# State-space stage of a transformer kernel: scan results transposed on TensorE and weighted by C columns on their way out of PSUM

## The reference, cut to what matters

```python
x = jnp.einsum('ed,bld->bel', in_proj_w, hidden_states)
xc = conv(x, conv_w)                       # depthwise, 4 taps
u = jax.nn.silu(xc + conv_b)
x_dbl = jnp.einsum('ke,bel->bkl', x_proj_w, u)
dt_lo, Bm, Cm = x_dbl[:, :DR], x_dbl[:, DR:DR + DS], x_dbl[:, DR + DS:]     # DR = 8, DS = 16
delta = softplus(einsum('er,brl->bel', dt_proj_w, dt_lo) + dt_proj_b)
A = -jnp.exp(A_log)
def step(state, xs):                       # over the 256 tokens; state is (b, 256 channels, 16)
    d_t, B_t, C_t, u_t = xs
    state = state * jnp.exp(d_t[..., None] * A) + (d_t * u_t)[..., None] * B_t[:, None, :]
    return state, jnp.einsum('ben,bn->be', state, C_t)
y = (scan of step) + D[None, :, None] * u
y = y * jax.nn.silu(z)
x = x + tanh(g_xattn[0]) * swap(y)
```

## Time and profile before

| | us |
|---|---|
| median of 3 runs | 1043.12 |
| lowest, highest | 1041.15, 1044.63 |
| span of the profiled execution (first to last instruction) | 1042.2 |
| of it, the state-space stage up to the next stage's first instruction | 160.2 |
| of that, first scan to end of last scan | 39.7 to 150.8 |

### The profile page before, as it was taken

The page is one execution under the profiler, slowest core; times in us unless marked ns, Lnnn a source line. Parts: engine busy times, 40 slices in busy tenths (PEclk is TensorE's granted clock), DMA queues, the critical chain, the costliest instruction groups (busy, mean ns, idle before and its releaser), DMA issues. The chain is left out here.

```text
span 1042.2 us, 16671 instructions
## 1 busy us (share of the span) xinstructions
PE 871.7 (84%) x5342; PEld 522.6 (50%) x5348; DVE 726.8 (70%) x1420; ACT 582.1 (56%) x1113; POOL 384.8 (37%) x329
## 2 busy tenths in 40 slices
PE   9456566989999999999499488999749999957787
PEld 4122223643577777777277373333425666645445
DVE  5999996788866676666768768997452324138875
ACT  5534442588677777777466365888403343205462
POOL 0366640068545555454133172000012766310132
PEclk9699997999999999999799899999969999979989
DMA  3321107400000000000000100400294332240001
GB/s 97 124 80 61 60 1 285 159 11 11 12 20 15 20 21 17 20 15 6 5 1 2 57 1 14 151 23 2 59 347 125 71 78 44 36 116 1 1 0 42
DMA packets 44348, 57.64 MB, mean 55 GB/s; under 512 B 5672, under 2 KB 35120, under 8 KB 44288
## 3 DMA queue, kind: packets, MB, share of 16 engines
q1 hardware_dynamic: 37792, 48.72, 13.9%
q0 software_dynamic: 4416, 6.03, 3.5%
q10 hardware_dynamic: 2080, 2.10, 0.6%
HBM read 50.29 MB, written 6.49 MB: 54 GB/s over the span
## 5 line engine op out<-in xcount | busy, mean ns | idle before, releaser
L1345 POOL TENSOR_TENSOR a_scratch<-a_scratch,a_inverse 128x512 f32<-128x512 f32 x64 | 66.5, 1039 | 115.3 <-DVE a_inverse L1481 115.3
L521 POOL TENSOR_TENSOR ssm_drive<-ssm_du,ssm_b_row 128x1024 f32<-128x1024 f32 x31 | 72.9, 2351 | 66.0 <-DVE ssm_state L596 33.2
L392 PE MATMUL bank<-ssm_seen,ident 128*128 128x512 f32 x128 | 63.3, 619 | 24.9 <-DVE ssm_seen L606 24.9
L2558 PE MATMUL bank<-wup,moe_xT 128*128 x184 | 83.0, 594 | 1.2 <-issue 0.6
L2342 DVE TENSOR_REDUCE a_tops<-bank 128x4 f32<-128x1024 f32 x64 | 77.7, 1223 | 8.5 <-PE bank L2022 5.5
L2793 DVE TENSOR_TENSOR moe_act_f<-bank,moe_silu 128x512 f32<-128x512 f32 x23 | 15.9, 692 | 92.7 <-ACT moe_silu L2627 80.6
L479 ACT ACTIVATE bank<-ssm_delta,ssm_a_neg 128x510 f32<-128x510 f32 x64 | 44.1, 690 | 63.7 <-DVE ssm_state L596 63.7
L2190 ACT ACTIVATE wup<-bank,a_exp_scale 128x1024 f32<-128x1024 f32 x64 | 71.1, 1113 | 13.8 <-PE bank L2045 13.8
L596 DVE TENSOR_TENSOR_SCAN ssm_state<-bank,ssm_drive 128x512 f32<-128x512 f32 x64 | 74.8, 1210 | 2.9 <-POOL ssm_drive L521 0.2
L1264 ACT ACTIVATE a_scratch<-bank,a_bias,a_q_factor 128x256 f32<-128x256 f32 x128 | 71.1, 559 | 7.1 <-DVE a_bias L1468 6.8
L1076 PE MATMUL bank<-keys,a_scratch 128*128 (+1 forms) x256 | 69.1, 392 | 1.6 <-DVE xn L1408 0.7
(11 more groups left out here) (499 smaller groups left out, 2203.6 us busy)
## 6 DMA issues: line engine op xcount, KB each, us to landing
ssm_b_row<-ssm_b_spill SPq DMA_DIRECT2D x16, 512.0 KB, 3.6
wup<-in_l_up_dram SPq DMA_DIRECT2D x8, 1024.0 KB, 9.5
a_wq_in<-in_l1x_q_dram SPq DMA_DIRECT2D x32, 128.0 KB, 2.1
wdn<-in_l_down_dram SPq DMA_DIRECT2D x8, 512.0 KB, 10.5
keys<-in_l1x_o_dram SPq DMA_DIRECT2D x1, 2048.0 KB, 10.9
X<-in_x_dram SPq DMA_DIRECT2D x1, 1024.0 KB, 6.9
lora_raw<-in_l_gate_dram SPq DMA_DIRECT2D x1, 1024.0 KB, 6.9
lora_raw<-in_l_up_dram SPq DMA_DIRECT2D x1, 1024.0 KB, 8.9
```

The source lines that it names most:

```text
L392: last = pe.matmul(bank[:, 4 + 2 * k + h, :], core.ident[:, :], seen[:, k, h * HALF:(h + 1) * HALF], start=False, stop=m >= STEPS - CC, sk ...
L521: pool.tensor_tensor(drive[:, k, :], du[:, k, :], b_row[:, n % NROW, :], ALU.mult).then_inc(S["drive_ready"], 1)
L1345: pool.tensor_tensor(prob[:, j, :, :], prob[:, j, :, :], inverse[:, j, :].unsqueeze(2).to_broadcast([P, 2, SEQ]), ALU.mult).then_inc(S["p_ ...
L2558: last = pe.matmul(bank[:, 2 * (i % 2) + m, :], xT[:, i % 2, c, :], wup[:, bass.ds(e, 1), c * 2 * FF + m * FF:c * 2 * FF + (m + 1) * FF] . ...
```

## The change

- Each unit of a column is now turned: TensorE transposes four 128x128 pieces of `state` (two tiles of 128 tokens by two chunks), a "round", into one PSUM bank (`turn`, banks 2 and 3 in turns). A column has four rounds. Time then stands on partitions, so that C is a column of factors, one per partition (`c_cols`, made once by eight small transposes and one copy on ScalarE).
- The bank is emptied through a multiplication by that column: rounds 0, 1 and 2 by ScalarE in two activations of 128x256 with a per-partition scale, round 3 by VectorE in one 128x512 multiplication (`weigh`). In the last column VectorE takes round 2 as well.
- `gather` adds the result with one 512-column matmul per round. The sum stands with time on partitions, so the transposes at the end go, and the skip term is now 16 matmuls of 128 columns.
- `c_rows`, the three bf16 parts and the load of the selection matrix go. So does `see`.
- z: GpSimd normalises the eight tiles behind drives 6 to 13 (`normal`). TensorE turns them in four extra rounds, one behind each of the columns 8 to 11, ScalarE copies them out (`bring_z`), and applies silu at the end. VectorE multiplies sum, gate and silu(z) into `gated`, and GpSimd adds that to `X`.
- `drive` has four buffers, `state` four (two columns by two chunks), `seen` four of half the size.

```diff
-    NROW = 4
+    NROW, NDRIVE, NSEEN = 4, 4, 4
     STEPS = CC * NS
+    ROUNDS = NT // 2
+    Z_STEP = 8
...
-select3 = s.sb("select3", [96, NS * P], BF16)
-parts, minus = s.sb("parts", [96, NTOK], BF16), s.sb("minus", [P, P], BF16)
-sixteenth, nmean, log_var = s.sb("sixteenth", [P, 1]), s.sb("nmean", [P, NT]), s.sb("log_var", [P, NT])
+c_cols = s.sb("c_cols", [P, NS, NT])
+sixteenth, log_var = s.sb("sixteenth", [P, 1]), s.sb("log_var", [P, NT])
...
-drive = s.sb("drive", [P, 2, NTOK])
-state = s.sb("state", [P, 2, NTOK])
-seen = s.sb("seen", [P, 2, NTOK])
+drive = s.sb("drive", [P, NDRIVE, NTOK])
+state = s.sb("state", [P, 2, CC, NTOK])
+seen = s.sb("seen", [P, NSEEN, HALF])
...
-silu_z = s.sb("silu_z", [P, NT, DM])
+z_turned = s.sb("z_turned", [P, NT // 2, HALF])
+gated = s.sb("gated", [P, NT // 2, HALF])
...
+rounds = []
+for n in range(NS):
+    rounds += [(n, r) for r in range(ROUNDS)] + [(n, "z")] * (Z_STEP <= n < Z_STEP + ROUNDS)
+place = {q: i for i, q in enumerate(rounds)}
+by_vector = lambda q: q[1] == 3 or q == (NS - 1, 2)
+emptied = {q: sum(by_vector(o) == by_vector(q) for o in rounds[:place[q] + 1]) for q in rounds}
+ring = lambda q: 2 + place[q] % 2
+def await_emptied(engine, q):
+    engine.wait_ge(S["dve_emptied" if by_vector(q) else "act_emptied"], emptied[q])
...
-        sp.dma_start(select3[:, :], d["select3"][:, NS * P:2 * NS * P]).then_inc(S["s_s"], 16)
...
-        pe.wait_ge(S["minus_ready"], 1)
-        for i in range(2):
-            rows = slice(2 * NS * i, 2 * NS * (i + 1))
-            pe.wait_ge(S["part_ready"], i + 1)
-            pe.wait_ge(S["rows_ready"], 1)
-            for h in range(2):
-                last = pe.matmul(bank[0:2 * NS, 2 + h, :], minus[rows, rows], parts[rows, h * HALF:(h + 1) * HALF],
-                                 start=False, stop=True, skip_group_check=True)
-            last.then_inc(S["part_out"], 1)
-        pe.wait_ge(S["part_ready"], 3)
-        pe.wait_ge(S["s_s"], 16)
-        def c_rows(n):
-            if n >= 1:
-                pe.wait_ge(S["seen_ready"], CC * n)
...
-        def gather(m):
-            k = m % CC
-            pe.wait_ge(S["seen_ready"], m + 1)
...
-        c_rows(0)
-        for n in range(NS):
-            gather(CC * n)
-            if n + 1 < NS:
-                c_rows(n + 1)
-            gather(CC * n + 1)
-        for b in range(NB):
-            pe.wait_ge(S["y_ready"], 3 + b // 2)
-            for h in range(2):
+        def skip_term(r):
+            for t in (2 * r, 2 * r + 1):
                 for k in range(CC):
-                    last = pe.transpose(bank[:, b, h * DM + k * P:h * DM + (k + 1) * P],
-                                        seen[:, k, b * SEQ + h * P:b * SEQ + (h + 1) * P], core.ident[:, :])
-            last.then_inc(S["y_turned"], 1)
+                    at = t % 2 * DM + k * P
+                    pe.matmul(bank[:, 4 + r, at:at + P], u[:, k, t * P:(t + 1) * P], skip_diag[:, k, :],
+                              start=t % 2 == 0 and k == 0, stop=False, skip_group_check=True)
+        skip_term(0)
+        skip_term(1)
+        pe.wait_ge(S["rows_ready"], 1)
+        for t in range(NT):
+            last = pe.transpose(bank[:, 2, t * 2 * NS:(t + 1) * 2 * NS], x_rows[:, t * P:(t + 1) * P],
+                                core.ident[0:2 * NS, 0:2 * NS])
+        last.then_inc(S["c_turned"], 1)
+        pe.wait_ge(S["positive_ready"], CC)
+        skip_term(2)
+        skip_term(3)
+        pe.wait_ge(S["c_ready"], 1)
+        def turn(q):
+            n, r = q
+            if place[q] >= 2:
+                await_emptied(pe, rounds[place[q] - 2])
+            if r == "z":
+                pe.wait_ge(S["z_normal"], NT)
+            else:
+                pe.wait_ge(S["scanned"], 4 * n + 3 + r // 2)
+            for j in range(2):
+                for k in range(CC):
+                    if r == "z":
+                        src = core.xn[:, 2 * (n - Z_STEP) + k, j * P:(j + 1) * P]
+                    else:
+                        src = state[:, n % 2, k, (2 * r + j) * P:(2 * r + j + 1) * P]
+                    last = pe.transpose(bank[:, ring(q), j * DM + k * P:j * DM + (k + 1) * P], src, core.ident[:, :])
+            last.then_inc(S["turned_round"], 1)
+        def gather(n, r):
+            await_emptied(pe, (n, r))
+            pe.matmul(bank[:, 4 + r, :], core.ident[:, :], seen[:, (4 * n + r) % NSEEN, :],
+                      start=False, stop=n == NS - 1, skip_group_check=True).then_inc(S["gathered"], 1)
+        for q, before in zip(rounds, [None] + rounds[:-1]):
+            turn(q)
+            if before is not None and before[1] != "z":
+                gather(*before)
+        gather(*rounds[-1])
...
+        act.wait_ge(S["c_turned"], 1)
+        act.copy(c_cols[:, :, :], bank[:, 2, 0:NT * 2 * NS].rearrange("p (t n) -> p n t", t=NT)[:, NS:2 * NS, :]
+                 ).then_inc(S["c_ready"], 1)
...
-        def centre(t):
-            act.activation(core.xn[:, t, :], core.X[:, t, :], ACT.Identity, bias=nmean[:, t:t + 1]
-                           ).then_inc(S["centred"], 1)
...
+        def weigh(n, r):
+            act.wait_ge(S["turned_round"], place[n, r] + 1)
+            await_count(act, S["gathered"], 4 * n + r - NSEEN + 1)
+            if (n, r) == (0, 0):
+                act.wait_ge(S["c_ready"], 1)
+            for j in range(2):
+                last = act.activation(seen[:, (4 * n + r) % NSEEN, j * DM:(j + 1) * DM],
+                                      bank[:, ring((n, r)), j * DM:(j + 1) * DM], ACT.Copy,
+                                      scale=c_cols[:, n, 2 * r + j:2 * r + j + 1])
+            last.then_inc(S["act_emptied"], 1)
+        def bring_z(n):
+            act.wait_ge(S["turned_round"], place[n, "z"] + 1)
+            act.copy(z_turned[:, n - Z_STEP, :], bank[:, ring((n, "z")), :]).then_inc(S["act_emptied"], 1)
+        decay(0)
+        for n in range(NS):
+            for r in range(3):
+                decay(4 * n + r + 1)
+                if n >= 1:
+                    weigh(n - 1, r)
+            if n + 1 < NS:
+                decay(4 * n + 4)
+            if n >= 1 and (n - 1, "z") in place:
+                bring_z(n - 1)
+        for r in range(2):
+            weigh(NS - 1, r)
         act.preload_act_table_set("silu_and_others")
-        act.wait_ge(S["root"], 1)
-        for t in range(NT):
-            act.wait_ge(S["centred"], t + 1)
-            act.activation(silu_z[:, t, :], core.xn[:, t, :], ACT.Silu, scale=core.rstd[:, t:t + 1]
-                           ).then_inc(S["silu_z_done"], 1)
         act.wait_ge(S["gates_s"], 3 * 16)
-        act.activation(core.gates[:, :], raw_gates[:, :], ACT.Tanh).then_inc(S["silu_z_done"], 1)
+        act.activation(core.gates[:, :], raw_gates[:, :], ACT.Tanh).then_inc(S["gates_ready"], 1)
+        act.wait_ge(S["act_emptied"], emptied[NS - 1, 1])
+        for r in range(ROUNDS):
+            act.activation(z_turned[:, r, :], z_turned[:, r, :], ACT.Silu).then_inc(S["silu_z_done"], 1)
...
+            if m >= NDRIVE:
+                pool.wait_ge(S["scanned"], 2 * (m - NDRIVE) + 2)
+            pool.tensor_tensor(drive[:, m % NDRIVE, :], du[:, k, :], b_row[:, n % NROW, :], ALU.mult
+                               ).then_inc(S["drive_ready"], 1)
+        def normal(t):
+            pool.wait_ge(S["root"], 1)
+            pool.tensor_scalar(core.xn[:, t, :], core.X[:, t, :], core.meanvar[:, t, 0:1], core.rstd[:, t:t + 1],
+                               ALU.subtract, ALU.mult).then_inc(S["z_normal"], 1)
         for m in range(1, STEPS):
             if m == CC:
                 pool.wait_ge(S["first_drive"], 1)
             drives(m)
+            if CC * (Z_STEP - 5) <= m < CC * (Z_STEP - 5) + NT:
+                normal(m - CC * (Z_STEP - 5))
+        for r in range(ROUNDS):
+            pool.wait_ge(S["y_ready"], r + 1)
+            pair = core.X[:, 2 * r:2 * r + 2, :].rearrange("p t n -> p (t n)")
+            pool.tensor_tensor(pair, pair, gated[:, r, :], ALU.add)
...
-        def see(m):
-            n, k = m // CC, m % CC
-            dve.wait_ge(S["scanned"], 2 * m + 2)
-            dve.wait_ge(S["c_done"], n + 1)
-            if m >= 2:
-                dve.wait_ge(S["summed"], m - 1)
-            dve.tensor_tensor(two(seen[:, k, :]), two(state[:, k, :]), bank[:, 2:4, :], ALU.mult
-                              ).then_inc(S["seen_ready"], 1)
...
+            if n >= 2:
+                dve.wait_ge(S["turned_round"], place[n - 2, 2 * h + 1] + 1)
+            dve.wait_ge(S["decay_ready"], i + 1)
+            dve.tensor_tensor_scan(state[:, n % 2, k, half], bank[:, h, :], drive[:, m % NDRIVE, half], 0.0,
+                                   ALU.mult, ALU.add).then_inc(S["scanned"], 1)
+        def weigh(n, r):
+            dve.wait_ge(S["turned_round"], place[n, r] + 1)
+            await_count(dve, S["gathered"], 4 * n + r - NSEEN + 1)
+            if n == 0:
+                dve.wait_ge(S["c_ready"], 1)
```

(18 more changed lines are left out.)

84 lines of the change are left out of this document (16 added, 68 removed).

## The result

The changed kernel takes 1026.37 us in the median of 4 runs (1025.94 to 1028.11), the kernel before beside it 1043.88: ratio 0.9841 (95%: 0.9823 to 0.9859): faster by 1.6%, clear of no change and under 2%. The forecast was 1029.5, a gain of 13.6 us, with a range of 1023 to 1040; the two series gave 17.5 and 14.5. The profiled execution took 1028.11 with a span of 1026.4, 15.8 less than before.

What follows compares the result with a forecast made beforehand. The prediction took VectorE alone as full in the loop of scans. The last scan ending 15.95 us earlier, less 2.36 given back in the tail, made -13.6 from 1043.1: 1029.5 us, range 1023 to 1040.

Steps and rivals of the forecast that it cites:

- What bounds it before, and the start: Loop of scans before: VectorE alone full; first scan unchanged at 39.72, the added skip and C work covered.
- Work per column: Loads per column in the changed loop: VectorE 5.29 us, TensorE 5.20, ScalarE 5.02, GpSimd 4.76, nearly equal.
- The ring: Loop: handovers from TensorE's `turn` through ScalarE to `gather` set 5.53 us per column, 6.83 with a round of z.
- columns 7 to 15: Late loop: four plain columns, four with z and the last column's scans take 54.12 us; last scan ends 134.82.
- Columns 0 to 6: Early loop: GpSimd's drives and eight `normal` decide; unit 14's drive is ready at 80.65, its scan starts at 80.70.
- Tail: Last scan to next stage: 11.78 us against 9.42 before, giving 2.36 back, mostly because GpSimd is last in line.
- After the stage: Rest of the program: nothing changed; TensorE idles about 3 us longer before the next stage's transposes, counted as 0.
- Sum: Whole program: -15.95 + 2.36 = -13.6 us, giving 1029.5.
- Rival 1: Loop: ScalarE's `weigh` and decays dearer, 5.99 us per column, 1035.3; chance 0.30 shared with Rival 2.
- Rival 2: Early loop: GpSimd's `normal` at 1.60 us, unit 14 comes 5.4 later, 1034.9; chance 0.30 shared with Rival 1.
- Rival 4: Loop: two handovers cost 0.45 us each, not 0.05; a column is 0.8 longer, 1042.3; chance 0.07.
- Rival 3: Loop: TensorE at 1.2 GHz, a column 10.4 us; five such columns make it 1054; chance 0.08.

Runs made afterwards that it cites:

- half_gather: Changed kernel with `seen` and the identity of `gather` in bf16, one pass per `gather` for two: 1020.81 us, ratio 0.9787 to the kernel before.
- no_normal: Changed kernel without GpSimd's eight normalisations, z turned from X as it is: 1024.12 us, ratio 0.9808 to the kernel before.
- after_again: The changed kernel itself, unaltered, measured again in a later series: 1028.06 us against 1042.55 for the kernel before, ratio 0.9864.
- z_scalar: Changed kernel with z turned ahead of the loop and all eight tiles normalised by ScalarE: 1019.06 us, ratio 0.9771 to the kernel before.
- no_z_rounds: Changed kernel without the four rounds of z in the loop, silu taken of X: 1025.25 us, ratio 0.9822 to the kernel before.

## Why the prediction was right, and where its sizes were off

- **What bounds it before, and the start.** Right: start 23.37 and 23.38, the skip matmuls and C columns were covered.
- **Work per column.** TensorE's load was put at 5.20 and is 5.19, VectorE's at 5.29 and is 5.16, because a scan after its `weigh` starts 0.58 later and not 0.77, while scans are 1.145 apart and not 1.13.
- **The ring, 5.53 per column.** Its size was off, and with that what binds plain columns: they are 5.15 to 5.19, and those with z 6.47 (6.83 forecast). ScalarE's two `weigh` and a decay start 1.34 apart (87.18, 88.52), so `weigh` is 0.365 to the next start and not 0.43 (recorded 0.475), and the `gather` that closes the ring has no wait before it, so its 0.10 falls away. With both the ring is 0.60 + 0.05 + (3 x 0.73 + 2 x 0.61 + 0.11 = 3.52) + 0.05 + 0.86 = 5.08, below TensorE's 5.19. The timeline agrees: the third pair of `weigh` is done at 90.70 (89.85 + 0.85), and its `gather` starts at 90.87, 0.12 after a handover of 0.05. So the ring doesn't bind plain columns; half_gather, in which TensorE has room, shows VectorE at 5.13. In columns with z the forecast had the right kind: handovers between TensorE and ScalarE decide, TensorE waits in them, and there the `gather` after the wait does cost 0.10 more (106.22 to 107.18, 0.96). But the handover that binds is the one behind `turn` 0: 0.60 + 0.04 + 0.84 + 0.05 + 0.96 + 0.44 + 0.90 + 0.44 + 0.90 + 0.44 + 0.86 = 6.47. The ring as forecast would be 5.08 + 1.30 = 6.38 with its corrected prices, only 0.09 below. The sizes were worth 1.45 us over four plain columns and 1.44 over four with z; columns 7 to 15 took 51.24 for 54.12.
- **Columns 0 to 6.** GpSimd decides, as said, and unit 14 starts 42.33 after the first scan for 40.98. A normalisation takes 1.21 to the next start for 0.93 (8 x 0.28 = 2.2 more), a drive 2.32 for 2.38 (14 x 0.06 = 0.8 less). no_normal confirms the place and the price. The two errors, -2.9 and +1.35, have opposite signs: that the loop's sum is off by 1.5 and not 2.9 is luck.
- **Tail.** 11.63 for 11.78, a `gather` and `turn` in 1.30 each, additions of 1.23 (4.93 for four).
- **After the stage.** No change of its own is shown; what the next stage gave (1.65) the rest took (1.68) in the profiled execution.
- **Sum.** -13.6 forecast, -15.3 for the stage. The median's gain of 17.5 is 2 us more than the stage's, and after_again's 14.5 is 1 less: the two lie on either side of the stage's, so the medians alone could not have told which terms were off.
- **Rival 1** (dearer ScalarE) fell: the price is below the one taken, not above. **Rival 2** held in part: normalisations 1.22, between 0.93 and 1.60. **Rival 4**: handovers are 0.03 to 0.06 (86.55 + 0.60, 87.18). **Rival 3** fell: the granted clock is 1.00 (2.4 GHz) from 50 us on, with `turn` recorded for 4.80 us and `gather` for 7.81 in 85 to 95 (the records overlap). The Trainium skill (TensorE: Matmul & The Clock Gate, Part 4) would have the transposes not count; in half_gather over 90 to 95 us transposes fill 2.34 us and gathers 1.04, and the clock is 1.00, so here they did no harm. The 0.50 at 70 to 75 us of that run, in which TensorE had both fewer passes and waits for GpSimd, doesn't tell the kind of its work from the amount, and that stays open.

## What to carry to other kernels

When one engine is full and the others are not, moving its work pays until the next one is full; here TensorE and VectorE met within 0.06 us a column (5.19 and 5.13), so further work in the loop cost time: a normalisation 0.6 us, half of its length, and a round of z 1.28, three times TensorE's work in it. The price of a round is its place in the order and the waits it opens, not its length alone. The next gain came from moving what the loop doesn't need into the idle time ahead of it. A price for work that leads (GpSimd's, with four buffers) has to be summed over the whole stretch, not per column. Divide by who waits for whom as well as by load: six to two between ScalarE and VectorE gave 5.2 per column, four to four 6.5.

## What the runs showed of the hardware that was not expected

- GpSimd and VectorE slow each other when both read SBUF alone. GpSimd's 128x256 normalisation took 1.22 us beside scans that read PSUM and SBUF, and 2.25 beside VectorE's operations with two operands in SBUF; those took 1.60 for 1.38 and 1.43 for 1.23. With GpSimd's work moved to ScalarE VectorE's operations took 1.38 and 1.23 (z_scalar); for GpSimd's side there is only the comparison with the loop. The Trainium skill (SBUF — State Buffer, section SBUF: two separate sides) says that the two share a port pair as an exclusive lock for whole instructions, when VectorE has two SBUF inputs and GpSimd reads SBUF. The rows agree that such instructions hold each other up, in the tail by 0.54 us where 0.68 overlapped. A lock for whole instructions they don't bear out: ahead of the loop VectorE's operations, 1.2 to 1.6 us long, overlapped GpSimd's all the way and grew by 0.15 to 0.22, or not at all.
- ScalarE with a factor per partition from PSUM, 128x256: 0.475 us recorded, the next starts after 0.36 to 0.37.
- The next stage takes 46.7 to 49.5 us with the same instructions, the longer ones with a granted clock of 0.50 from 5 to 10 us into it, and the statistics of X start between 15.78 and 17.18 us: between them 1 to 4 us of one execution's time that no edit of the stage is shown to explain. In the longest case, no_z_rounds, the granted clock was 0.67 over 145 to 155 us.
